# Gated cross-attention kernel: keys stored once, loads by broadcast, the split moved to GpSimd

## The chip, the cores and the metric

The kernel runs on one core of one Trainium2 chip. The metric is the device time of one execution in microseconds (us). A core has TensorE (PE, matmuls into PSUM), VectorE (DVE), ScalarE (ACT), GpSimd (POOL) and SyncE (SP, which here only issues DMAs); 16 DMA engines move the data between HBM and SBUF. Engines meet at semaphores.

## The reference, cut to what matters

```
x = x + tanh(g_xattn) * xattn(layernorm(x), ctx)      # x: 8 x 512 x 256, ctx: 8 x 1601 x 128
x = x + tanh(g_ffn)   * ffn(layernorm(x))

xattn:  q, k, v = x@Wq+bq, x@Wk+bk, x@Wv+bv           # 16 heads of 16
        y  = softmax(causal(q k^T / 4)) v
        qc, kc, vc = x@Wcq+bcq, ctx@Wck+bck, ctx@Wcv+bcv
        y += softmax(qc kc^T / 4) vc
        return y @ Wp + bp
ffn, twice:  weights = softmax over the 2 chosen of 6 experts
        combined  = sum_e weights[e] * (expert_e(xf) + bdown_e)
        share_out = sum over 2 shared experts of (... @ share_Wdown + share_bdown)
        xf = rmsnorm(xf + combined + share_out)
```

The weights of a token's two experts add up to 1.

## The kernel before, in words

A float32 operand is used as a high part of reduced width (the type F32R) and a low part, the difference; products of the two are summed, so that the result keeps float32's precision. The program has four stages, each a block that all engines leave together.

**Projection** (`stage_project`, 8 batches). PE makes queries, keys and values into six PSUM banks, by 23 outputs a batch, ten of them keys. Queries: DVE adds the bias (line 406) and SP stores one row set (`q_rows`). Keys: ACT writes the high part (line 479), DVE reads the same bank again and writes the low part (line 395), and SP stores both parts of every piece (`k_parts`, line 297, 8 DMAs a batch). Values: DVE adds the bias (line 420) and SP stores them at the batch's end (line 314). DVE also makes the low part of the next batch's context (`ctx_low`, line 381, both inputs in SBUF). Towards the end ACT issues the loads of the first item's rows (`First.load_rows`, one DMA for each 16 rows), and GpSimd splits the first item's queries (`split_queries`, lines 114 and 118).

**Attention** (`stage_attend`, 32 items: a batch's four groups of 4 heads). On the contracted axis PE sees 64 rows for each pair of heads: three copies of the 16 rows of a head (queries high, high, low against keys high, low, high), two rows that hold the softmax shift, and rows of zeros. Three key tiles and three query tiles rotate. The order of PE's work is written out by hand, one letter for a piece, and every item takes the same string:

```
ORDER = ("AMSMASMAMSAMSMASMAMSAMSMASMASMOSAMSMASMA"
         "SHAMSMASMAMSAMSMASMAMSAMSMASMAMSAMSMASMA"
         "MSAMSMAASHMASMMSAASMMSMSASMOSA")
```

S are scores (line 893, exponentials by ACT at line 850), A the product with the values (line 908), M the maximum tiles of the next item (line 881, reduced by DVE at line 803), O the output of the item before (self part) or of this one (cross part). H transposes maxima into shift rows: the first H is the self part of this item, the second the cross part of the next. After each H, DVE writes the rows and SP moves them into the query tile with four small DMAs, each from 8 partitions (`shift_rows`, line 687); PE's first scores of that part wait for them. These first cross scores are the last two S of the string.

SP's queue in one item, in this order: keys of item n+2 (`load`, 18 DMAs, line 664), values of n+2, zeros for the scatter rows, a block of x every fourth item (line 722), the self shift of n, queries of n+3 (`load_queries`, 12 DMAs, line 675), the output of n-1 (`store`), the cross shift of n+1. GpSimd's queue: copy of the values of n+1 (line 759), split of the queries of n+2, four causal masks (line 786), the sum of item n's two outputs (line 792).

**Mix** (`stage_mix`): output projection, residual from `XR`, layernorm, routing, preparation of the expert weights and of the bias rows `BR`. **Experts** (`stage_experts`): two layers of routed blocks and of shared passes; a shared down projection begins with a bf16 matmul of a selector row with the bias (line 2051), 64 times in all.

Of the kernel before, what the change touches and what calls it, by code (L numbers as in the profile page):

```python
# [17 lines left out]
P = 128  # L18
# [22 lines left out]
KPART = [0, 1, 0]  # L41
# [65 lines left out]
def written(tag, batches):  # L107

    return (32 if tag[0] in "kc" else 16) * batches + 1


def split_queries(pool, q, raw, s_hi, s_lo, n):

    pool.tensor_copy(q[:, :, :, :], raw[:, :, :, :]).then_inc(s_hi, 1)
    pool.wait_ge(s_hi, n + 1)
    for h in range(2):
        rows = slice(64 * h + 2 * D, 64 * h + 3 * D)
        pool.tensor_tensor(q[rows, :, :, :], raw[rows, :, :, :], q[rows, :, :, :].bitcast(F32), ALU.subtract).then_inc(s_lo, 1)  # L118
    pool.wait_ge(s_lo, 2 * n + 2)
# [45 lines left out]
class First:  # L165


    def __init__(self, r_):
        self.K, self.Q = r_.sb("K0", [P, 2, NKE], F32R), r_.sb("Q0", [P, 2, 2, T], F32R)
        self.qraw = r_.sb("qraw", [P, 2, 2, T])  # L170
# [4 lines left out]
        self.s_qld, self.s_hi, self.s_lo = r_.sem("qld"), r_.sem("qhi"), r_.sem("qlo")  # L175
        self.s_wr = {n: r_.sem("wr_" + n) for n in WRITES}

    def clear(self, pool):

        pool.memset(self.zero[:, :, :, :], 0.0).then_inc(self.s_fill, 1)  # L180
        pool.memset(self.mx[:, :, :], 0.0).then_inc(self.s_fill, 1)
        for h in range(2):
            pool.wait_ge(self.s_fill, h + 2)
            pool.memset(self.K[64 * h + 32:64 * h + 64, :, :].bitcast(F32), 1.0).then_inc(self.s_fill, 1)
        pool.wait_ge(self.s_fill, 4)

# [8 lines left out]
    def load_rows(self, eng, h, r, QS, KS):  # L195

        rows = slice(64 * h + r * D, 64 * h + (r + 1) * D)
        eng.dma_start(self.K[rows, :, 0:NK].bitcast(F32),
                      KS[KPART[r]].rearrange("(i p h d) c -> i h d p c", i=NI, p=2, h=2)[0, h]).then_inc(self.s_ld, 16)
# [8 lines left out]
def stage_project(nc, a, QS, KS, VS, const, first):  # L208
    with ExitStack() as ctx:
# [14 lines left out]
        kpart = r_.sb("kpart", [P, 2, KC, NK], F32R)  # L224
# [30 lines left out]
        NSP = len(split)  # L255

# [12 lines left out]
        r_.prime({s_fin.name: NO})  # L269
        with nc.Block() as block:  # L270

            @block.sync
            def _(sp):
# [11 lines left out]
                def write(b, tag):  # L285
# [4 lines left out]
                    sp.wait_ge(s_fin, NO * (b + 1) + ks[-1] + 2)  # L290
# [4 lines left out]
                    for part in range(2):  # L295
                        row = KS[part].rearrange("(b r) c -> b r c", b=B)[bass.ds(b, 1), cg * P:(cg + 1) * P, c0:c0 + n]
                        sp.dma_start(row.rearrange("o r c -> (o r) c"), tile[:, part, cg, c0:c0 + n].bitcast(F32)).then_inc(s_wr[tag], 16)
# [5 lines left out]
                def body(b, more, more2):  # L303
# [8 lines left out]
                    sp.wait_ge(s_fin, NO * (b + 2) + 1)  # L312
# [11 lines left out]
            def _(pool):  # L324
# [15 lines left out]
                for n in range(4, B):  # L340
                    power(n)
                pool.wait_ge(first.s_qld, 16 * 14)
                split_queries(pool, first.Q, first.qraw, first.s_hi, first.s_lo, 0)

            @block.vector
            def _(dve):
# [36 lines left out]
                def body(b, more):  # L383
                    for k, o in enumerate(outs):
# [7 lines left out]
                        if k in rank:  # L392
                            tile, cg, c0, n, bias = parts(o)
                            dve.wait_ge(s_h, b * NSP + rank[k] + 2)
                            dve.scalar_tensor_tensor(tile[:, 1, cg, c0:c0 + n], bank[:, 0:n], bias,
                                                     tile[:, 0, cg, c0:c0 + n].bitcast(F32), ALU.add, ALU.subtract
                                                     ).then_inc(s_fin, 1)
# [42 lines left out]
            def _(act):  # L440
# [22 lines left out]
                def body(b, more, early=None):  # L463
                    seen = set()
                    for k, o in enumerate(outs):
# [9 lines left out]
                        if o[3] not in seen:  # L475
                            act.wait_ge(s_wr[o[3]], 32 * b + 1)
                            seen.add(o[3])
                        act.wait_ge(s_out, b * NO + k + 2)
                        act.activation(tile[:, 0, cg, c0:c0 + n], acc[k % NBANK][:, 0:n], ACT.Identity,
# [18 lines left out]
            def _(pe):  # L498
# [10 lines left out]
                def body(b, more):  # L509
                    for k, o in enumerate(outs):  # L510
# [10 lines left out]
                        prev = k - NBANK if k >= NBANK else max(i for i in range(NO) if i % NBANK == k) - NO  # L521
                        pe.wait_ge(s_fin, NO * (b + 1) + prev + 2)
# [34 lines left out]

def stage_attend(nc, a, QS, KS, VS, YS, XS, XR, idf, idm, mqm, first, early):

# [5 lines left out]
    with ExitStack() as ctx:  # L565
# [18 lines left out]
        s_ld = [r_.sem(f"ld{u}") for u in range(NU)]  # L584
# [1579 lines left out]
```

## Time and profile before

| | us |
|---|---|
| median of 3 runs | 2416.43 |
| lowest and highest | 2416.25, 2420.34 |
| the profiled execution, its own time | 2420.15 |
| its span, first to last instruction | 2418.1 |

The profiled execution lies 3.7 us over the median, and 2.1 us of its time lie outside its span. Times inside the span count from its start. The stages end at about 213.5, 1575 and 1678 us; the first 39.5 us of attention work on the maxima of item 0.

### The profile page before, as it was taken

How to read it: one execution, taken by the hardware profiler on the slowest of the kernel's cores; microseconds unless marked ns; L12 is line 12 of the kernel's file. 1: busy time of each engine (PE TensorE's matmuls, PEld its weight loads, DVE VectorE, ACT ScalarE, POOL GpSimd, SP SyncE). 2: the span in 40 equal slices, each digit the busy share in tenths (PEclk: the TensorE clock that was granted, in tenths of full speed). 3: DMA queues.
4: the chain of work that ended last, by engine and by line, in shares of the span. 5: the costliest groups of instructions: out<-in, count | busy, mean ns of one | idle time of the engine just before them, and what ended most of it. 6: DMA issues, size and time to landing. Idle time of an engine off the chain costs nothing. (4 is left out here: it accounts for less than half of the span.)

```text
span 2418.1 us, 56126 instructions
## 1 busy us (share of the span) xinstructions
PE 2319.9 (96%) x20518; PEld 1485.7 (61%) x20518; DVE 1892.7 (78%) x3186; ACT 1556.5 (64%) x3328; POOL 814.8 (34%) x631
## 2 busy tenths in 40 slices
PE   7978999999999999999999999988999999999996
PEld 7866444444444444444444444487888888888885
DVE  7869899999999999999999999476633654654747
ACT  3321688888888888888888888854344543533542
POOL 0205343333334242424243332023332423523514
PEclk9997899999999999999999999987999999999998
DMA  7999554545464645454444543262144422422623
GB/s 280 385 338 304 97 101 87 102 77 95 83 98 73 95 82 85 89 86 89 85 86 88 92 73 58 61 213 71 65 137 125 136 68 87 142 70 85 206 82 110
DMA packets 176970, 289.25 MB, mean 120 GB/s; under 512 B 48775, under 2 KB 115470, under 8 KB 175310
## 3 DMA queue, kind: packets, MB, share of 16 engines
q1 hardware_dynamic: 163358, 249.03, 43.7%
q0 software_dynamic: 12288, 33.57, 4.5%
q8 instruction: 166, 2.72, 0.5%
q10 hardware_dynamic: 1072, 3.23, 0.5%
q14 instruction: 86, 0.70, 0.1%
HBM read 165.10 MB, written 119.29 MB: 118 GB/s over the span
## 5 line engine op out<-in xcount | busy, mean ns | idle before, releaser
L850 ACT ACTIVATE at_P<-at_ST 128x512 f32<-128x512 f32 (+4 forms) x2176 | 1091.5, 557 | 233.8 <-PE at_ST L893 189.2
L803 DVE TENSOR_REDUCE f_part<-at_R 128x2 f32<-128x804 f32 x1024 | 953.6, 990 | 43.8 <-PE at_R L881 26.5
L908 PE MATMUL at_OP<-at_P,at_V 128*32 128x256 f32 x8192 | 621.7, 383 | 3.5 <-ACT at_O L858 0.8
L893 PE MATMUL at_ST<-at_Q,at_K 64*128 64x512 f32 (+4 forms) x1428 | 324.8, 428 | 1.3 <-ACT at_P L850 0.9
L908 PEld LDWEIGHTS at_OP<-at_P,at_V 128*32 128x32 f32 x8192 | 172.8, 108 | 248.9 <-ACT at_P L850 186.0
L881 PE MATMUL at_R<-at_K,at_Q 64*128 64x402 f32 x1344 | 273.1, 401 | 0.0
L893 PEld LDWEIGHTS at_ST<-at_Q,at_K 64*128 64x128 f32 (+1 forms) x1428 | 155.0, 181 | 127.5 <-ACT at_P L850 114.5
L800 DVE TENSOR_REDUCE f_mx<-at_R 128x2 f32<-128x256 f32 (+3 forms) x256 | 204.4, 820 | 34.9 <-PE at_R L874 29.3
L786 POOL TENSOR_SCALAR_AFFINE_SELECT at_P<-at_P 128x512 f32<-128x512 f32 x128 | 81.2, 634 | 405.0 <-ACT at_P L850 405.0
L1881 DVE TENSOR_TENSOR ex_ab<-ex_bank,ex_sg 128x256 f32<-128x256 f32 x148 | 62.8, 425 | 195.0 <-ACT ex_sg L1964 177.4
L881 PEld LDWEIGHTS at_R<-at_K,at_Q 64*128 64x128 f32 x1344 | 126.3, 184 | 140.4 <-DVE f_part L803 106.3
L1043 POOL DMA_INDIRECT sorted<-c_XR,c_IDX x128 | 126.7, 989 | 218.4 <-DVE c_bcmp L1119 88.2
L1824 POOL DMA_INDIRECT ex_gb<-expert_rows,c_IDX x128 | 127.0, 992 | 206.7 <-DVE ex_ab L1881 115.4
L118 POOL TENSOR_TENSOR at_Q<-f_qraw,at_Q 16x2048 fp32r<-16x2048 f32 x42 | 191.8, 4568 | 3.3
L1964 ACT ACTIVATE ex_sg<-ex_bank 128x256 f32<-128x256 f32 x148 | 56.8, 384 | 184.6 <-PE ex_bank L100 184.6
L792 POOL TENSOR_TENSOR at_ysum<-at_y 128x256 f32<-128x256 f32 x32 | 23.4, 733 | 443.6 <-DVE at_y L829 443.6
L893 PE MATMUL at_ST<-f_Q,f_K 64*128 64x512 f32 (+4 forms) x748 | 170.2, 430 | 0.5 <-ACT at_P L850 0.5
L881 PE MATMUL at_R<-f_K,f_Q 64*128 64x402 f32 x704 | 151.3, 426 | 9.1 <-DVE f_part L803 6.5
L98 PE MATMUL ex_bank<-c_WH,ex_xbL 128*128 x296 | 143.7, 486 | 0.0
L881 PEld LDWEIGHTS at_R<-f_K,f_Q 64*128 64x128 f32 x704 | 68.8, 192 | 88.7 <-DVE f_part L803 70.4
L893 PEld LDWEIGHTS at_ST<-f_Q,f_K 64*128 64x128 f32 (+1 forms) x748 | 81.3, 183 | 64.6 <-ACT at_P L850 61.2
L100 PE MATMUL ex_bank<-c_WH,ex_xbH 128*128 x296 | 117.0, 395 | 0.0
(250 smaller groups left out, 4425.3 us busy)
## 6 DMA issues: line engine op xcount, KB each, us to landing
k_parts<-pj_kpart SPq DMA_DIRECT2D x32, 800.5 KB, 7.5
f_qraw<-q_rows SPq DMA_DIRECT2D x372, 64.0 KB, 2.8
at_K<-k_parts SPq DMA_DIRECT2D x252, 88.0 KB, 5.2
expert_rows<-ex_rb SPq DMA_DIRECT2D x148, 128.0 KB, 1.7
ex_xb<-sorted SPq DMA_DIRECT2D x72, 256.0 KB, 3.1
v_items<-pj_vbuf SPq DMA_DIRECT2D x8, 2176.0 KB, 11.7
at_K<-k_parts SPq DMA_DIRECT2D x126, 88.1 KB, 5.6
f_K<-k_parts SPq DMA_DIRECT2D x120, 88.0 KB, 5.1
```

The lines of the kernel that those rows point to most:

```text
L98: pe.matmul(out, wL, xH, start=start, stop=False)
L100: return pe.matmul(out, wH, xH, start=False, stop=stop)
L118: pool.tensor_tensor(q[rows, :, :, :], raw[rows, :, :, :], q[rows, :, :, :].bitcast(F32), ALU.subtract).then_inc(s_lo, 1)
L786: pool.affine_select(out=diag, in_=diag, compare_op=ALU.is_ge, fill=0.0, base=0, pattern=[[0, G], [1, P]], channel_multiplier=-1).then_inc ...
L800: dve.tensor_reduce(maxima(SELF)[:, :, p, q], buf[:, :, 0:(q + 1) * P], AX.X, ALU.max).then_inc(s_drain, 1)
L803: dve.tensor_reduce(part[:, :, p, q, c], buf[:, :, 0:XC], AX.X, ALU.max).then_inc(s_drain, 1)
L850: act.activation(Pt[(NKT * n + s) % NP][0:rows, h, c0:T], ST[(NST * n + s * G + h) % NB][0:rows, c0:T], ACT.Exp, scale=SCALE).then_inc(s_e ...
L881: ins = pe.matmul(buf[:, h, 0:XC], Q[u][r0:r0 + 64, CROSS, p, q * P:(q + 1) * P], K[u][r0:r0 + 64, p, at:at + XC], start=True, stop=True)
L893: pe.matmul(ST[t % NB][0:rows, c0:T], K[n % NU][half, p, keys], Q[n % NU][half, kind, p, c0:T], start=True, stop=True).then_inc(s_st, 1)
L908: ins = pe.matmul(OP[32 * h:32 * h + 2 * D, at], V[n % 2][0:rows, key_tile(s), h, :], Pt[(NKT * n + s) % NP][0:rows, h, at], start=s in (0 ...
L1043: pool.indirect_dma_start(XS[h], bass.IndirectOffsetOnAxis(ap=self.IDX[h][:, j, t:t + 1], axis=0), XR[:, h * self.HT + t, :], None).then_i ...
L1824: pool.indirect_dma_start(gb[n % NGB][j][:, :], None, RS[h], bass.IndirectOffsetOnAxis(ap=R.IDX[h][:, j, t:t + 1], axis=0)).then_inc(s_ga[ ...
```

## The change

The keys are stored once, in float32, and so are no longer split in the projection. In attention a raw key tile takes three identical copies of each row set by a broadcast DMA, and GpSimd splits it with two instructions into the tile that PE reads; queries are loaded and split in the same way. A column `low` of 0 and 1 picks the rows that take the low part. One raw tile of each kind serves all items, so its next load waits for the split before it. GpSimd's sum of an item's outputs moves to the next item, between the two splits. SP now issues the keys of item n+3 behind the self shift of n, and the queries behind the store, both ahead of the cross shift of n+1. `load_rows`, for item 0, keeps its DMAs. The blocks of x are loaded in the mix stage. The shared down bias is added, twice, to each expert's down bias, so the matmul at line 2051 goes.

```diff
-KPART = [0, 1, 0]
+KPART = [1, 0, 0]
+def split_rows(pool, out, raw, low, s_hi, s_lo, done):
+    pool.tensor_scalar(out, raw, low, 1.0, ALU.mult, ALU.mult).then_inc(s_hi, 1)
+    pool.wait_ge(s_hi, done)
+    pool.tensor_tensor(out, raw, out.bitcast(F32), ALU.subtract).then_inc(s_lo, 1)
+    pool.wait_ge(s_lo, done)
...
+    def split_keys(self, pool, K, n):
+        split_rows(pool, K[:, :, 0:NK], self.kraw[:, :, 0:NK], self.low[:, 0:1], self.s_hi, self.s_lo, 2 * n + 1)
+    def split_queries(self, pool, Q, n):
+        split_rows(pool, Q[:, :, :, :], self.qraw[:, :, :, :], self.low[:, 1:2], self.s_hi, self.s_lo, 2 * n + 2)
...
@@ projection: SP, GpSimd, DVE
-                    for part in range(2):
-                        row = KS[part].rearrange("(b r) c -> b r c", b=B)[...]
-                        sp.dma_start(row.rearrange("o r c -> (o r) c"), tile[:, part, cg, c0:c0 + n].bitcast(F32)).then_inc(s_wr[tag], 16)
+                    row = KS.rearrange("(b r) c -> b r c", b=B)[...]
+                    sp.dma_start(row.rearrange("o r c -> (o r) c"), tile[:, cg, c0:c0 + n]).then_inc(s_wr[tag], 16)
...
+                pool.wait_ge(s_xn, QT * B + 1)
+                pool.wait_ge(first.s_ld, 16 * 6)
+                first.split_keys(pool, first.K, 0)
                 pool.wait_ge(first.s_qld, 16 * 14)
-                split_queries(pool, first.Q, first.qraw, first.s_hi, first.s_lo, 0)
+                first.split_queries(pool, first.Q, 0)
...
                         if k in rank:
-                            dve.scalar_tensor_tensor(tile[:, 1, cg, c0:c0 + n], bank[:, 0:n], bias, ...
                             continue
@@ attention: SP
                 def load(n):
-                    for r in range(3):
-                        for h in range(2):
-                            for c0, c1 in zip(KCUT, KCUT[1:]):
-                                sp.dma_start(K[u][rows, :, c0:c1].bitcast(F32), KS[KPART[r]]...[n, h, :, :, c0:c1]).then_inc(s_ld[u], 16)
+                    sp.wait_ge(first.s_lo, 2 * n - 1)
+                    src = KS.rearrange("(i p h d o) c -> i p h o d c", i=NI, p=2, h=2, o=1)
+                    for p in range(2):
+                        for h in range(2):
+                            sp.dma_start(first.kraw[64 * h:64 * h + 3 * D, p, 0:NK],
+                                         src[n, p, h].to_broadcast([3, D, NK])).then_inc(first.s_ld, 16)
                 def load_queries(n):
                     sp.wait_ge(first.s_lo, 2 * n)
                     for h in range(2):
-                        for r in range(3):
-                            for kind in range(2):
-                                sp.dma_start(first.qraw[rows, kind], q[n, h, kind]).then_inc(first.s_qld, 16)
+                        for p in range(2):
+                            sp.dma_start(first.qraw[64 * h:64 * h + 3 * D, :, p], q[n, h, p].to_broadcast([3, D, 2, T])
+                                         ).then_inc(first.s_qld, 16)
...
                 shift_rows(0, CROSS)
+                load(2)
                 load_queries(2)
                 for n in range(NI):
                     if n + 2 < NI:
-                        load(n + 2)
                         load_values(n + 2)
                     clear(n)
-                    if n % NG == 1:
-                        sp.dma_start(XR[:, b * QT:(b + 1) * QT, :], ...).then_inc(s_xr, 16)
                     shift_rows(n, SELF)
                     if n + 3 < NI:
-                        load_queries(n + 3)
+                        load(n + 3)
                     if n >= 1:
                         store(n - 1)
+                    if n + 3 < NI:
+                        load_queries(n + 3)
                     if n + 1 < NI:
                         shift_rows(n + 1, CROSS)
@@ attention: GpSimd
+                keys(1)
                 queries(1)
                 for n in range(NI):
                     if n + 1 < NI:
                         values(n + 1)
+                    if n + 2 < NI:
+                        keys(n + 2)
+                    if n:
+                        both(n - 1)
                     if n + 2 < NI:
                         queries(n + 2)
                     ...
@@ mix and experts
+                load_x(0)
                 load_y(1)
+                load_x(1)
...
+                        dve.scalar_tensor_tensor(raw[:, 2, :], sbias[:, :], float(NS), raw[:, 2, :], ALU.mult, ALU.add)
...
-                        pe.matmul(dst, SEL[:, NE, :], BR[:, 2 * C:3 * C], start=True, stop=False)
```

## Rows read from the trace of the kernel before

**Rows 1.** Windows by stage: us; busy PE, PEld, DVE, ACT, POOL; clock; DMA share; GB/s

```profile
0.00:213.50 213.50, 178.29 (x1048) 160.46 (x1048) 167.63 (x382) 71.92 (x112) 32.66 (x34) 0.96 0.94 339
...
253.00:1575.00 1322.00, 1312.51 (x14475) 625.59 (x14475) 1194.73 (x1526) 1123.27 (x2239) 464.92 (x280) 1.00 0.49 85
...
1678.00:2418.00 740.00, 707.78 (x4251) 600.84 (x4251) 416.44 (x1029) 309.85 (x868) 259.50 (x261) 0.98 0.35 109
```

**Rows 2.** A window inside the projection stage

```profile
60.00:70.00 10.00, 10.00 (x56) 8.71 (x55) 9.81 (x25) 2.31 (x3) 1.82 (x2) 1.00 1.01 415
```

**Rows 3.** Timeline of SP in the projection stage

```profile
45.58 1.65 SPq L293 DMA_DIRECT2D q_rows<-pj_qpart  x2
...
66.68 1.65 SPq L293 DMA_DIRECT2D q_rows<-pj_qpart  x2
...
198.87 1.65 SPq L293 DMA_DIRECT2D q_rows<-pj_qpart  x2
```

**Rows 4.** Timeline of SP in one item of attention

```profile
602.12 2.66 SPq L687 DMA_DIRECT2D at_Q<-at_sh  x4
...
620.02 2.66 SPq L687 DMA_DIRECT2D f_Q<-at_sh  x4
...
643.41 2.00 SPq L687 DMA_DIRECT2D f_Q<-at_sh  x3
```

**Rows 5.** Timeline of PE: the first cross scores of the next item

```profile
624.83 0.50 PE L893 MATMUL at_ST<-f_Q,f_K 64*128 64x512 f32 x2
```

**Rows 6.** DMA issues: KB each, median us to landing

```profile
k_parts<-pj_kpart SPq DMA_DIRECT2D x32, 800.5 KB, 7.5
f_qraw<-q_rows SPq DMA_DIRECT2D x372, 64.0 KB, 2.8
at_K<-k_parts SPq DMA_DIRECT2D x252, 88.0 KB, 5.2
...
k_parts<-pj_kpart SPq DMA_DIRECT2D x32, 256.0 KB, 8.7
```

**Rows 7.** DMA packets of 601.5 to 609 us: only the four shift DMAs

```profile
DMA packets 65, 0.03 MB, mean 4 GB/s; under 512 B 32, under 2 KB 64, under 8 KB 64
```

**Rows 8.** DMA packets of 611 to 619.6 us: 12 query loads, one store

```profile
DMA packets 1104, 0.92 MB, mean 107 GB/s; under 512 B 720, under 2 KB 720, under 8 KB 1104
```

**Rows 9.** Timeline of POOL at the end of the projection stage

```profile
184.57 1.89 POOL L114 CAST f_Q<-f_qraw 128x2048 fp32r<-128x2048 f32 x1 [19.94 <-DMA f_qraw<-q_rows]
186.54 9.29 POOL L118 TENSOR_TENSOR f_Q<-f_qraw,f_Q 16x2048 fp32r<-16x2048 f32 x2
```

**Rows 10.** Line 381 alone: its durations in ns, min, median, max

```profile
L381 DVE TENSOR_TENSOR pj_ctxL<-pj_ctxr,pj_ctxH x8: 1806/1814/4379, 16.8 to 193.1; 128x1602 fp32r<-128x1602 f32 x8
```

**Rows 11.** Timeline of POOL in one item of attention

```profile
618.94 0.64 POOL L786 TENSOR_SCALAR_AFFINE_SELECT at_P<-at_P 128x512 f32<-128x512 f32 x1 [7.48 <-ACT at_P L850]
...
624.96 0.64 POOL L786 TENSOR_SCALAR_AFFINE_SELECT at_P<-at_P 128x512 f32<-128x512 f32 x1 [0.55 <-ACT at_P L850]
639.85 0.73 POOL L792 TENSOR_TENSOR at_ysum<-at_y 128x256 f32<-128x256 f32 x1 [14.25 <-DVE at_y L829]
640.52 1.09 POOL L759 COPY at_V<-f_vraw 128x1088 f32<-128x1088 f32 x1
```

**Rows 12.** Windows around PE's stall in the projection stage

```profile
182.00:184.00 2.00, 1.80 (x5) 1.79 (x6) 2.00 (x6) 0.33 (x1) 0.00 (x0) 0.50 0.99 353
184.00:186.00 2.00, 2.00 (x7) 1.90 (x7) 2.00 (x4) 1.25 (x3) 1.43 (x1) 0.50 0.93 365
186.00:188.00 2.00, 2.00 (x14) 2.00 (x14) 2.00 (x5) 0.80 (x2) 1.92 (x2) 0.76 0.91 334
```

**Rows 13.** Instructions of at_Q: first and last start

```profile
L893 PE MATMUL at_ST<-at_Q,at_K x1428: 219/397/504, 294.6 to 1570.2; 64*128 64x512 f32 x136, 64*65 64x512 f32 x11, 64*128 64x384 f32 x11, 64*128 64x128 f32 x11
L881 PE MATMUL at_R<-at_K,at_Q x1344: 335/441/683, 253.1 to 1525.8; 64*128 64x402 f32 x192
```

**Rows 14.** Groups of instructions, the line that goes in the experts stage

```profile
L2051 PE MATMUL ex_bank<-c_BR,c_SEL 96*128 96x256 bf16 x64 | 18.4, 287 | 6.0 <-DVE ex_aL L1860 6.0
```

More of the change, by code:

```diff
@@ L169, in __init__ @@
         self.K, self.Q = r_.sb("K0", [P, 2, NKE], F32R), r_.sb("Q0", [P, 2, 2, T], F32R)
-        self.qraw = r_.sb("qraw", [P, 2, 2, T])
+        self.qraw, self.kraw = r_.sb("qraw", [P, 2, 2, T]), r_.sb("kraw", [P, 2, NKE])
+        self.low = r_.sb("low", [P, 2])
         self.vraw = r_.sb("vraw0", [P, NKT, GC])
@@ L183, in clear @@
             pool.wait_ge(self.s_fill, h + 2)
-            pool.memset(self.K[64 * h + 32:64 * h + 64, :, :].bitcast(F32), 1.0).then_inc(self.s_fill, 1)
+            pool.memset(self.kraw[64 * h + 32:64 * h + 64, :, :], 1.0).then_inc(self.s_fill, 1)
         pool.wait_ge(self.s_fill, 4)
+        pool.memset(self.low[:, :], 0.0).then_inc(self.s_fill, 1)
+        done = 5
+        for kind, parts in enumerate((KPART, QPART)):
+            for h in range(2):
+                r0 = 64 * h + parts.index(1) * D
+                pool.wait_ge(self.s_fill, done)
+                pool.memset(self.low[r0:r0 + D, kind:kind + 1], 1.0).then_inc(self.s_fill, 1)
+                done += 1
+        pool.wait_ge(self.s_fill, done)
+    def split_keys(self, pool, K, n):
+        split_rows(pool, K[:, :, 0:NK], self.kraw[:, :, 0:NK], self.low[:, 0:1], self.s_hi, self.s_lo, 2 * n + 1)
+    def split_queries(self, pool, Q, n):
+        split_rows(pool, Q[:, :, :, :], self.qraw[:, :, :, :], self.low[:, 1:2], self.s_hi, self.s_lo, 2 * n + 2)
     def load_zeros(self, eng):
@@ L255, in stage_project, with finished @@
         NSP = len(split)
+        plain = [k for k, o in enumerate(outs) if o[0] not in "kc"]
+        place = {k: j for j, k in enumerate(plain)}
+        NPL = len(plain)
+        def finished(k, b):
+            return (s_h, NSP * (b + 1) + rank[k] + 2) if k in rank else (s_fin, NPL * (b + 1) + place[k] + 2)
         def parts(o):
@@ L554, in _, with stage_attend @@
                 body(B - 1, False)
-def stage_attend(nc, a, QS, KS, VS, YS, XS, XR, idf, idm, mqm, first, early):
+def stage_attend(nc, a, QS, KS, VS, YS, XS, idf, idm, mqm, first, early):
     with ExitStack() as ctx:
@@ L762, in queries, with keys @@
                 def queries(n):
-                    pool.wait_ge(first.s_qld, 16 * (14 + QLOADS * n))
                     if n >= NU:
                         pool.wait_ge(s_st, NST * (n - NU + 1))
-                    split_queries(pool, Q[n % NU], first.qraw, first.s_hi, first.s_lo, n)
-                ones(1)
+                    pool.wait_ge(first.s_qld, 16 * (14 + QLOADS * n))
+                    first.split_queries(pool, Q[n % NU], n)
+                def keys(n):
+                    if n >= NU:
+                        pool.wait_ge(s_st, NST * (n - NU + 1))
+                    pool.wait_ge(first.s_ld, keys_in(n))
+                    first.split_keys(pool, K[n % NU], n)
                 for n in WRITES:
```

130 lines of the change are left out of this document (52 added, 78 removed).

## The prediction

> **What bounds the kernel now.** I read the windows by stage first. The projection is at its DMAs' limit: 213.5 us with 339 GB/s and a DMA share of 0.94 [rows 1]. Inside it a full stretch moves 415 GB/s at a share of 1.01 [rows 2], so one of the 16 engines moves 25.9 GB/s. The SP timeline tells what a batch costs without that: the shortest distance between two batches' query stores is 21.1 us, while the seven distances from 22.15 to 198.87 average 25.2 [rows 3]. Attention is PE's: 1312.5 of 1322 us, clock 1.00 [rows 1], one item in 41.3 us (the self shifts at 602.12 and 643.41 [rows 4]). PE's order is fixed, so anything that PE waits for is added in full. Its tightest link is the cross shift: SP issues its four DMAs at 620.02 to 622.68 [rows 4], and PE's first scores that read them start at 624.83 [rows 5]. A DMA takes some 2.6 us beyond its transfer (a 64 KB load lands after 2.8 [rows 6], of which 0.2 at 415 GB/s), so there is next to no slack.
>
> **How a load is spread.** In 601.5 to 609 us only the four shift DMAs run, each from 8 source partitions. They leave 32 data packets and 32 small ones, 8 of each per DMA [rows 7]. Beside them 12 query loads to 16 partitions and one store from 128 leave 720 small packets, of which 512 are the store's 256-byte rows: 208 for 13 DMAs, 16 each [rows 8]. I read the small packet as one engine's completion. Then a DMA runs on as many engines, up to 16, as its outer dimension gives: 8 for 8 rows. The new loads' destination has 48 partitions, but their source begins with the broadcast dimension of 3, and a division that fits both gives 3. Bounds: 3 and 16 engines; I take 3, since the 8-row DMAs show the smaller side deciding (their destination is one row of 1024).
>
> The Trainium skill (DMA: Bandwidth & Descriptors, "Why a DMA increments its semaphore by 16 and not by 1") takes the largest number up to 16 that divides both outer dimensions, says that these are the lowest-numbered engines, and in its rules for kernel authors names a leading broadcast of c copies as confining a DMA to c engines. By that rule the new loads run on three engines; the trace agrees on 8 and 16 [rows 7, 8] and holds no case of 3.
>
> **The change, part by part** (against the profiled execution's 2420.15 us, 3.7 over the median).
>
> Projection. 213.5 us at 339 GB/s [rows 1] are 72 MB, 9.0 a batch; the key stores are 32 of 800.5 KB and 32 of 256 KB [rows 6], 4.3 MB a batch, and half of them goes. At 21.1 us a batch the remaining 6.9 MB need 325 GB/s, below the 415 seen. DVE loses ten low parts a batch. I keep the first distance of 23.4 (filling) and set the other six, 153.3 us from 45.58 to 198.87 [rows 3], to 21.1: 126.6, so -26.7. At the end GpSimd now splits item 0's keys before its queries. The query split shows 1.89 us for 2048 elements in one-input form and 4.6 in two-input form [rows 9]; for the keys' 4226 that is 3.9 + 9.4 = 13.3 us, and the queries fall to 1.9 + 4.6 = 6.5, one subtraction in place of two. The split's inputs were there at 184.57, and GpSimd had waited 19.9 us for them [rows 9]. The batch that issues them comes about 13 us earlier (half of the 26.7), and with short queues I take 4 more off: 167, so the split ends near 187, with the stage (213.5 - 26.7). The price of `tensor_scalar` has no row: bounds are the one-input and the two-input rate, 3.9 and 9.4 us; I take 3.9, since it reads one tensor. I book -26, bounds -12 and -32.
>
> One danger lies here. Line 381 takes 1814 ns, but 4379 the one time it met GpSimd's subtraction [rows 10]: begun at 193.14, it ran on past that one's end at 195.83 [rows 9]. The keys' subtraction is a 9.4 us obstacle of this kind; it stands inside the bound of -12.
>
> The Trainium skill (SBUF — State Buffer, "Who interferes with whom") says that a DVE instruction with two SBUF inputs and a GpSimd one that reads SBUF lock each other out for a whole instruction. By it the projection could lose up to 9.4 us more, and attention nothing, because DVE's instructions there have at most one input in SBUF; rows 10 agree for the first, and no row quoted here shows the second.
>
> Attention, GpSimd. Its queue gets, an item, values 1.1 + keys 13.3 + sum 0.7 + queries 6.5 before the masks. It is free at 625.6 behind the last mask and needs until about 649 (PE's products with values a little later than the mask included), and the next first mask would come at 618.94 + 41.3 = 660.2 [rows 11]: 11 us of slack, 3 if both `tensor_scalar` cost the two-input rate. I book 0. The sum's move is hidden as well: its store is waited for two items later.
>
> Attention, the loads. Their bytes don't change: 18 x 88 KB and 12 x 64 KB [rows 6], 1.62 and 0.79 MB. Three engines carry 77.8 GB/s: 20.9 and 10.1 us. SP now issues both between the self shift of n and the cross shift of n+1. With the self shift's issue as zero [rows 4]: its DMAs are out at 2.7, the keys (the split before them being done) follow, the queries behind them; all has landed at 2.7 + 2.6 + 31.0 = 36.3. The cross shift is issued at 17.9 as before, but its packets stand behind the loads on the three engines, which it also uses. It lands at 36.5 instead of before 22.7, and **PE waits 13.8 us an item**. After a stall PE works at half clock: in the projection line 395 and its like began again at about 182, and the clock was still 0.50 to 186 and 0.76 on average to 188 [rows 12]: some 4.8 us at half speed, 2.4 lost. Together 16.2 us an item, for n = 1 to 28 (no key load follows item 31): 28 x 16.2 = 454. Bounds per item: 12 (clock free) and 27 (engines a third slower when alone).
>
> Attention, the first items. Against the stage's start T (213.5 before): loads of item 1 land at T + 34.3, splits end at T + 54.1, and PE wants item 1's maxima at 253.1 [rows 13], T + 39.6: +14.5. The keys of item 2 wait for that key split (T + 47.6), their own split ends at T + 84.4, and SP holds the keys of item 3, their queries and the cross shift of item 1 behind it: landing at T + 118. PE wanted it at 294.6 [rows 13], T + 81.1. So +37 for n = 0, the 14.5 included. SP's queue is blocked there by the wait for the split: behind it stand the store and the cross shift.
>
> Mix and experts. The x blocks come from a DMA in the stage, needed well behind its start: 0 to 3, I take +1. One broadcast and one DVE operation on the bias: 0. Line 2051 goes 64 times. Its group's 18.4 us overlap other matmuls [rows 14]; the stage's 4251 matmuls take 707.8 us [rows 1], 0.17 each, so 64 are 10.7. This one is bf16 and 256 wide, narrower than most: -6, bounds 0 and -11.
>
> **Sum:** 2420.15 - 26 + 37 + 454 + 1 - 6 = 2880 us, 19% slower.
>
> **The rivals.**
> (1) The loads use all 16 engines after all, by their 48 partitions. Then keys and queries have landed at 2.7 + 2.6 + 5.8 = 11, before the cross shift is issued, and what stays is 2420.15 - 26 - 6 + 1 = 2389, faster. The point that decides is the landing at 22.7: 2.41 MB in 17.4 us are 138 GB/s, between five and six engines. For it: I have no row with 3. Against it: rows 7.
> (2) Three engines, but small DMAs overtake the loads. Then only the first items' 14.5 stay: 2404. Against it: nothing in the trace lets a later DMA pass.
> (3) Three engines, each slower alone than in a full stretch, or a clock that recovers later: each us more costs 28; a fifth slower is 6 us or 174: 3050 and up.
> (4) The gain of the projection is eaten by a lock or a late load, with (1): 2420.
>
> **How the numbers follow.** The forecast has 0.72, rival (1) 0.15, (2) 0.02, (3) 0.09, (4) 0.02. The predicted time is the forecast's. Its own range is 2720 to 3060 by the bounds above; to 3180 it takes in most of (3) and holds nearly 8 in 10. The two faster cases stay outside. Faster by over 0.2% (what a measurement here can tell): 0.17; within: 0.02; slower: 0.81.
>
> **What would show it.** Small packets per broadcast load: 3, against 16. In attention DMA share near 0.2 while loads run; PE idle 14 us an item in front of line 893, ended by the DMA at_Q<-at_sh, clock below 1.00, items of 57 us. In the projection, query stores 21 us apart and a stage end near 187. GpSimd: 3.9 + 9.4 us for a key split. I am wrong if the items stay at 41.3 us.

## The result: 3127.53 us, and the profile after

The changed kernel took 3127.53 us (median of 4 runs, 3116.30 to 3131.04) against 2416.51 us for the kernel before on the same chip. The ratio is 1.293, with a 95% interval of 1.291 to 1.295. The direction and the mechanism were forecast, and 2880 was 8% short. The profiled execution is the 3116.30 us one, with a span of 3114.6; before it was 2420.15 us. All of the loss lies in attention. Windows by stage of the kernel after, in the columns of [rows 1]:

```profile
0.00:190.50 190.50, 173.37 (x1048) 159.83 (x1048) 124.64 (x302) 71.43 (x112) 44.83 (x40) 0.99 0.85 298
237.00:2260.00 2023.00, 1352.22 (x14332) 643.52 (x14332) 1193.78 (x1521) 1116.24 (x2211) 737.40 (x309) 0.82 0.17 53
2370.00:3114.00 744.00, 707.67 (x4229) 605.25 (x4229) 422.81 (x1047) 314.31 (x877) 268.94 (x270) 0.98 0.36 110
```

The projection stage ends at 190.5 in place of 213.5. Attention's row is 2023 us long where [rows 1] has 1322. PE's busy time in it hardly grew, its clock fell to 0.82, and the DMA share is 0.17 on average. What PE waited for is in the waits view (engine, line, what it waited for; us in total, times, the longest):

```profile
PE at_ST L906 <- DMA at_Q<-at_sh: 445.4, 20, 27.5
PE at_ST L906 <- DMA f_Q<-at_sh: 210.7, 11, 23.8
PE at_R L894 <- POOL at_Q L116: 15.7, 1, 15.7
```

656.1 us over 31 waits end with the shift DMA. The third row is the split of item 1, once. One item in full, on SP (start and duration, us), which answers to [rows 4]:

```profile
1844.39 2.69 SPq L699 DMA_DIRECT2D f_Q<-at_sh  x4
1847.13 3.04 SPq L678 DMA_DIRECT2D f_kraw<-k_rows  x4
1850.22 0.58 SPq L704 DMA_DIRECT2D y_rows<-at_ysum  x1
1850.85 25.58 SPq L686 DMA_DIRECT2D f_qraw<-q_rows  x4
1876.47 4.28 SPq L699 DMA_DIRECT2D at_Q<-at_sh  x4
...
1909.04 2.69 SPq L699 DMA_DIRECT2D at_Q<-at_sh  x4
```

and PE's first score that reads the cross shift:

```profile
1889.17 0.79 PE L906 MATMUL at_ST<-at_Q,at_K 64*128 64x512 f32 x2 [22.04 <-DMA at_Q<-at_sh]
```

The self shift is issued at 1844.39 and the cross shift can be used at 1889.17, which is +44.8 where it was +22.7 before [rows 4, 5] and 36.5 was forecast. PE had stood for 22.0 us. The four query loads alone kept SP for 25.58 us, where a DMA's issue otherwise takes 0.7. Windows through the same item:

```profile
1857.00:1863.00 6.00, 5.92 (x74) 2.93 (x74) 5.35 (x9) 4.85 (x10) 0.64 (x1) 1.00 0.20 63
1869.00:1875.00 6.00, 0.00 (x0) 0.00 (x0) 0.00 (x0) 0.00 (x0) 0.00 (x0) 0.50 0.18 69
1887.00:1891.00 4.00, 1.83 (x18) 1.31 (x18) 0.32 (x1) 1.00 (x2) 0.00 (x0) 0.50 0.08 31
1891.00:1895.00 4.00, 3.98 (x42) 1.72 (x44) 3.14 (x5) 2.99 (x7) 1.90 (x2) 0.79 0.00 0
1895.00:1899.00 4.00, 4.00 (x46) 1.75 (x46) 3.88 (x6) 3.53 (x7) 3.92 (x2) 1.00 0.02 4
```

While the loads run, 0.18 to 0.20 of sixteen engines are busy, three, and they move 63 to 69 GB/s, all transfers included, and not the 77.8 of the sum. The granted clock is at half (1.2 GHz) while PE stands and stays there for some 4 us after its restart. The packet row of the DMA view, for the 64 us of one item (1842 to 1906):

```profile
DMA packets 1468, 3.45 MB, mean 54 GB/s; under 512 B 664, under 2 KB 728, under 8 KB 1240
```

Its small packets are counted against another kernel's below.

### The profile page after: what moved, and what is told of

Its sections match the earlier page's. It is cut to its first block and busy times, and to the rows that moved or that the text cites. A ratio compares the mean times of both kernels' runs of the same rounds, so it can differ in the third digit from the quotient of the medians.

```text
span 3114.6 us, 55137 instructions
## 1 busy us (share of the span) xinstructions
PE 2360.8 (76%) x20454; PEld 1506.2 (48%) x20454; DVE 1848.8 (59%) x3107; ACT 1561.7 (50%) x3328; POOL 1079.5 (35%) x663
## 5 line engine op out<-in xcount | busy, mean ns | idle before, releaser
L906 PE MATMUL at_ST<-at_Q,at_K 64*128 64x512 f32 (+4 forms) x1428 | 332.9, 448 | 446.3 <-DMA at_Q<-at_sh 445.4
L921 PE MATMUL at_OP<-at_P,at_V 128*32 128x256 f32 x8192 | 642.4, 396 | 3.3 <-ACT at_O L871 0.8
L894 PE MATMUL at_R<-at_K,at_Q 64*128 64x402 f32 x1344 | 276.6, 407 | 15.7 <-POOL at_Q L116 15.7
L116 POOL TENSOR_TENSOR at_K<-f_kraw,at_K 128x4226 fp32r<-128x4226 f32 x21 | 193.9, 9236 | 1.7
L759 POOL COPY at_V<-f_vraw 128x1088 f32<-128x1088 f32 x16 | 17.5, 1092 | 380.7 <-PE at_OP L921 380.7
L759 POOL COPY at_V<-at_vraw 128x1088 f32<-128x1088 f32 x16 | 17.5, 1092 | 362.1 <-PE at_OP L921 362.0
```

The source lines that it names most:

```text
L116: pool.tensor_tensor(out, raw, out.bitcast(F32), ALU.subtract).then_inc(s_lo, 1)
L894: ins = pe.matmul(buf[:, h, 0:XC], Q[u][r0:r0 + 64, CROSS, p, q * P:(q + 1) * P], K[u][r0:r0 + 64, p, at:at + XC], start=True, stop=True)
L906: pe.matmul(ST[t % NB][0:rows, c0:T], K[n % NU][half, p, keys], Q[n % NU][half, kind, p, c0:T], start=True, stop=True).then_inc(s_st, 1)
L921: ins = pe.matmul(OP[32 * h:32 * h + 2 * D, at], V[n % 2][0:rows, key_tile(s), h, :], Pt[(NKT * n + s) % NP][0:rows, h, at], start=s in (0 ...
```

## Where the 696 us come from

SP's self shifts are the clock of attention. Those of items 0, 1 and 29 in the kernel after, and the cross shift behind the last:

```profile
280.25 3.72 SPq L699 DMA_DIRECT2D f_Q<-at_sh  x4
...
349.28 2.65 SPq L699 DMA_DIRECT2D at_Q<-at_sh  x4
...
2171.30 2.69 SPq L699 DMA_DIRECT2D at_Q<-at_sh  x4
2189.16 2.67 SPq L699 DMA_DIRECT2D f_Q<-at_sh  x4
```

From the self shift of item 1 (349.28) to that of item 29 (2171.30) 28 items take 65.07 us each. Before it is 41.3 [rows 4]. The cross shift behind 2171.30 comes 17.86 us later, as before: there no load stands in between. The self shift of item 1 stands 158.8 us behind the start of the stage, and 99.7 before (313.18 - 213.5 in the timeline of SP). From the self shift of item 29 to the end are 943.3 us, against 948.5 before (from 313.18 + 28 x 41.3 = 1469.6 to 2418.1).

| part | predicted | measured |
|---|---|---|
| projection | -26 | -23 |
| first items | +37 | +59.1 |
| 28 items | 28 x 16.2 = +454 | 28 x 23.8 = +665.6 |
| mix and experts | +1 - 6 = -5 | -5.2 |
| sum from 2420.15 | 2880 | 3116.6 (3116.3 measured) |

## The experiments

Where a run has a single time, that time is its profiled execution's. The items' lengths are means over the 28 items from the self shift of item 1 to that of item 29, as above; the changed kernel has 65.07.

The kernel before was timed beside every group of runs. It took 2413.73 to 2422.76 us beside the first four experiments, 2415.44 to 2421.59 beside the half rows and the last experiment, and 2416.33 beside the rows 32 partitions apart. But beside the other four (queries by copy, ScalarE's cross shift, the cross shift ahead of the loads, copies 0 and 1 in pairs) its only execution took 2472.31 us, 55 more than usual. It left no trace, but the four show the like: from the last self shift (item 31) to the end they take 909 to 915 us, all other kernels here 860 to 867, the changed kernel 862. No edit touches that part, so 47 to 52 us of each of these four times have nothing to do with the experiment. Their items can be compared, their totals only with this in mind.

### One DMA per copy

```
-                    for p in range(2):
-                        for h in range(2):
-                            sp.dma_start(kraw[64h : 64h+48, p, 0:NK], src[n, p, h].to_broadcast([3, D, NK]))
+                    for r in range(3):
+                        for h in range(2):
+                            sp.dma_start(kraw[64h+16r : 64h+16r+16, :, 0:NK], src[n, h])
```

The queries are treated likewise, 12 DMAs in place of 4.

> One DMA per copy of 16 rows (6 for the keys, 12 for the queries of an item) in place of four broadcasts each; all else as in the changed kernel. Three-engine theory: each load runs on 16 engines again, cross shifts land some 23 us after the self shift's issue, items fall from 67.4 to 41.3 us, DMA rate while loads run is far above 77.8 GB/s, the time is 2385 (2370 to 2405). Rival, the split on GpSimd or its waits cost the time: it stays above 3000 and GpSimd's key splits end late. Rival, the store-once loads are slow by their byte count: no change either.

Measured: 2524.13 us (5 runs, ratio 1.043, interval 1.041 to 1.045). So 603 of the 711 us of loss (3127.53 - 2524.13, of 3127.53 - 2416.51) go with the number of engines, and the rivals (GpSimd's split, SP's waits, the bytes, all unchanged) fall. But it is not 2385: items take 45.4 us. SP, a window, and PE in this kernel:

```profile
1028.99 2.66 SPq L700 DMA_DIRECT2D at_Q<-at_sh  x4
1031.95 2.68 SPq L678 DMA_DIRECT2D f_kraw<-k_rows  x6
...
1035.30 5.97 SPq L687 DMA_DIRECT2D f_qraw<-q_rows  x12
1046.86 2.67 SPq L700 DMA_DIRECT2D f_Q<-at_sh  x4
```

```profile
1033.00:1053.00 20.00, 18.84 (x220) 9.22 (x218) 17.56 (x23) 15.44 (x34) 3.46 (x5) 1.00 1.05 131
```

```profile
1054.67 0.79 PE L907 MATMUL at_ST<-f_Q,f_K 64*128 64x512 f32 x2 [1.82 <-DMA f_Q<-at_sh]
```

All sixteen engines are busy (share 1.05), and together they move only 131 GB/s, a third of the 415 of [rows 2]. The cross shift is issued on time, 17.9 us after the self shift, but lands at +25.7. Its 8452-byte packets take 1059 ns on average, against 320 to 330 for one that runs undisturbed. The kernel before does the same in its own key loads, to which no row of the prediction went:

```profile
626.00:640.00 14.00, 13.96 (x146) 6.48 (x147) 13.33 (x17) 12.69 (x24) 0.15 (x1) 1.00 1.04 121
```

The limit of such a load is thus neither the number of engines nor HBM (415 GB/s were seen with both). What these loads have in common is 16 neighbouring partitions as their destination. The Trainium skill (SBUF — State Buffer, "Door 1: The DMA port swizzle") says that DMA bandwidth depends on how many of 16 ports the partitions reach, with four neighbours on one port. By it 16 neighbours reach four ports, and with that page's 436 GB/s for all 16 a load into them gets 109 GB/s by estimate. The 121 and 131 measured lie 11% and 20% above that, other transfers included; the six key loads by themselves bring 1.62 MB in 13.6 us on average, 119 GB/s. The next experiment brings the same key bytes, on sixteen engines too, into 48 partitions a load, in 10.1 us. That fits a limit set by the partitions; no run varies the partitions alone.

### The copy as the inner dimension

```
-                            sp.dma_start(kraw[64h : 64h+48, p, 0:NK], src[n, p, h].to_broadcast([3, D, NK]))
+                            sp.dma_start(kraw[64h : 64h+48, p, 0:NK], src[n, p, h].to_broadcast([D, 3, NK]))
```

Row d's copy r now lies in partition 3d + r of its half, so the mask `low` and `load_rows` use every third partition. Queries likewise, with `qraw` laid out as pair, kind, column.

> The same 8 broadcasts an item, but the copy is the second dimension of the source (16 rows, 3 copies, the row) and row d's copy r lies in partition 3d + r of its half, so the outer dimension is 16. Three-engine theory: 16 small packets per load, items of 41.3 us, 2385 (2365 to 2405), within 0.5% of one DMA per copy. Rival, a broadcast is slow in itself, since it reads each row three times: it stays near 3116.

Measured: 2391.11 us (4 runs, ratio 0.988, interval 0.987 to 0.990). The same eight broadcasts, the same bytes and the same splits, and the time is 26.6 us under the kernel before. Items are at 41.30 us. It beats both kernels. SP and a window:

```profile
1033.17 2.66 SPq L701 DMA_DIRECT2D at_Q<-at_sh  x4
1035.87 2.54 SPq L680 DMA_DIRECT2D f_kraw<-k_rows  x4
...
1039.09 2.55 SPq L688 DMA_DIRECT2D f_qraw<-q_rows  x4
1051.03 2.76 SPq L701 DMA_DIRECT2D at_Q<-at_sh  x4
```

```profile
1035.00:1053.00 18.00, 17.92 (x204) 8.37 (x206) 16.86 (x23) 15.43 (x31) 4.79 (x3) 1.00 0.86 144
```

SP is no longer held: four query loads issue in 2.55 us. Packets of one item:

```profile
DMA packets 1382, 3.48 MB, mean 84 GB/s; under 512 B 768, under 2 KB 832, under 8 KB 1152
```

768 small packets against 664 in the changed kernel: 104 more, that is 8 loads x (16 - 3). So a load leaves 16 completions here and left 3 there, and the reading of [rows 7, 8] by which the source's leading 3 sets the number of engines holds.

### The bias change alone

Kernel before, with the shared experts' down bias added once to the routed rows' bias, and line 2051 gone.

```
-                        pe.matmul(dst, SEL[:, NE, :], BR[:, 2 * C:3 * C], start=True, stop=False)
                         for c in range(KC):
                             ins = mm3(pe, dst, aH[:, c, tok], aL[:, c, tok], dH[:, NE, c, :], dL[:, NE, c, :],
-                                      False, c == KC - 1)
+                                      c == 0, c == KC - 1)
```

> The kernel before with the shared down bias in the routed rows alone. By the prediction's term: 64 narrow bf16 matmuls less, -6 us (0 to -11), 2410 against 2416.4. Rival: they lay beside other work and nothing moves, 2416.

Measured: 2413.84 us against 2417.73 (ratio 0.998, interval 0.997 to 0.999), -3.9 us with an interval of -7 to -3. The experts stage shows it, 734 us and 4188 matmuls where [rows 1] has 740 and 4251:

```profile
1678.00:2412.00 734.00, 700.98 (x4188) 598.20 (x4187) 416.26 (x1031) 309.89 (x868) 260.33 (x261) 0.98 0.35 110
```

### Keys by copy, queries by broadcast

The keys' half of the first diff, the queries' broadcasts left as they are:

```
-FIRST, LOADS, QLOADS = 6, 4, 4
+FIRST, LOADS, QLOADS = 6, 6, 4
```

> Keys by six DMAs of 16 rows, queries still by four broadcasts. Three-engine theory: the queries need 10.1 us on three engines, begin at some 6 us after the self shift's issue and have landed by 21 us, ahead of the cross shift's 22.7: no stall, items of 41 to 43 us, 2390 (2380 to 2440). Rival, broadcasts hurt by being issued at all (SP blocked in issuing the queries whatever stands ahead): the 27 us of issue stay, items above 55, 2800 and more.

Measured: 2722.88 us, items of 52.1. A miss. SP:

```profile
999.67 2.77 SPq L678 DMA_DIRECT2D f_kraw<-k_rows  x6
...
1003.45 11.06 SPq L686 DMA_DIRECT2D f_qraw<-q_rows  x4
1014.82 5.04 SPq L699 DMA_DIRECT2D f_Q<-at_sh  x4
```

The expectation took 4 us for the keys by copy. At 121 GB/s their 1.62 MB need 13.4, and only then come the queries' 10 on three engines: 2.7 + 2.6 + 13.4 + 10.1 is 29, 6 over the limit of 22.7. The measured excess of an item is 10.8. PE's waits for shifts are 260.9 us in 29 waits, 9.0 each, where this sum has 6; the clock adds to them, and the rest is not resolved further. What decided here was the rate into 16 partitions, again. SP's issue shrank from 26 to 11 us, so the rival, that issuing a broadcast blocks SP whatever stands ahead, falls too.

### Queries by copy, keys by broadcast

The other half:

```
-FIRST, LOADS, QLOADS = 6, 4, 4
+FIRST, LOADS, QLOADS = 6, 4, 12
```

> Queries by twelve DMAs of 16 rows, keys still by four broadcasts. Three-engine theory with the measured keys (29 us on the slowest of the three): all has landed at 35 us after the self shift's issue, the cross shift at 36.5 in place of 46.5, items of 57.5 us in place of 67.4, 2840 (2780 to 2900). With three engines at the full 25.9 GB/s each the keys would need 20.9, items of 49 and 2600. Rival, most of the wait comes from the queries' broadcasts: items under 50 us, 2550 or less.

Measured: 3053.53 us, items of 61.0. A miss in size, also without the 47 us.

```profile
1023.62 2.81 SPq L700 DMA_DIRECT2D f_Q<-at_sh  x4
1026.48 3.03 SPq L678 DMA_DIRECT2D f_kraw<-k_rows  x4
...
1030.20 28.06 SPq L687 DMA_DIRECT2D f_qraw<-q_rows  x12
1058.30 2.78 SPq L700 DMA_DIRECT2D at_Q<-at_sh  x4
```

```profile
1066.07 0.80 PE L907 MATMUL at_ST<-at_Q,at_K 64*128 64x512 f32 x2 [19.66 <-DMA at_Q<-at_sh]
```

PE can use the cross shift at +42.5 (1066.07 - 1023.62), not +36.5. SP is held in issuing the queries for 28 us, although thirteen of the engines that they use have no keys to carry, so the cross shift is issued at +34.7. Nor do the keys get away with 29 us: the queries' packets now run beside them into the same partitions, the key packets' mean is 453 ns (395 in the changed kernel), and the last of this item's ends 33.6 us behind the start of the first. The expectation had priced neither. What holds SP was not tried by itself.

### ScalarE issues the cross shift

Loads unchanged. The four DMAs of the cross shift leave SP's queue for ScalarE's.

```
 # SP
-                    if n + 1 < NI:
-                        shift_rows(n + 1, CROSS)
 # ScalarE, two exponentials behind the SHIFT event of (n, CROSS)
+                    act.wait_ge(s_drain, slot["SHIFT", n, CROSS] + 1)
+                    for h in range(2):
+                        for r in range(2):
+                            row = 64 * h + KROWS + r
+                            act.dma_start(Q[n % NU][row:row + 1, CROSS].bitcast(F32),
+                                          sh[CROSS][2 * QT * h:2 * QT * (h + 1), r].bitcast(F32)).then_inc(s_shd[CROSS], 16)
```

> Cross shifts issued by ScalarE, in its own queue, two exponentials after their place; loads unchanged. Theory A, the cross shift waits behind the loads in SP's queue (27 us of issue and the packets ahead in it): out of that queue it lands within 5 us of its issue, items of 42 to 46 us, 2420 (2390 to 2530). Theory B, the engines are the shared thing and serve in order of issue over all queues: it waits for the loads all the same, items above 55 us, 2800 and more.

Measured: 2646.11 us, items of 47.1. SP is held as before, and an item's loads still take 39 us:

```profile
1033.84 2.80 SPq L699 DMA_DIRECT2D at_Q<-at_sh  x4
1036.68 3.05 SPq L678 DMA_DIRECT2D f_kraw<-k_rows  x4
...
1040.40 26.83 SPq L686 DMA_DIRECT2D f_qraw<-q_rows  x4
```

```profile
PE at_ST L918 <- DMA at_Q<-at_sh: 54.4, 20, 4.2
PE at_ST L918 <- DMA f_Q<-at_sh: 28.6, 11, 5.4
```

PE's 656 us of waits for shifts become 83. Out of SP's queue the cross shift passes the loads; the engines that both use are not the obstacle, the place in SP's queue is. The time is 116 us over the range, of which 52 lie behind attention. The 39 us of loads stand in one queue with the next self shift; with the 5.3 us from a shift's issue to the first byte behind it that makes 44 of the item's 47 us, so it is the loads' own length that is left. The expectation had left it out.

### SP issues the cross shift ahead of the loads

```
-                        load(n + 3)
                     if n >= 1:
                         store(n - 1)
-                    if n + 3 < NI:
-                        load_queries(n + 3)
                     if n + 1 < NI:
                         shift_rows(n + 1, CROSS)
+                    if n + 3 < NI:
+                        load(n + 3)
+                        load_queries(n + 3)
```

> SP issues the cross shift ahead of the key and query loads; they are unchanged. By queue order the cross shift lands 5 us after its issue, but the loads then take until 42 us behind it: the next self shift lands at 44 where PE can use it at 37, and the splits of those loads (13.3 and 6.5 us) end on GpSimd at 52, ahead of the item's masks. Items of 50 (self shift decides) to 60 us (masks decide), 2630 to 2900, I take 2850. Rival, the order is of no account: 3116.

Measured: 2806.90 us, items of 52.7. The stall moved to the next self shift, now the one that stands behind the loads:

```profile
1040.07 2.68 SPq L699 DMA_DIRECT2D f_Q<-at_sh  x4
1042.79 3.11 SPq L678 DMA_DIRECT2D f_kraw<-k_rows  x4
1045.94 23.55 SPq L686 DMA_DIRECT2D f_qraw<-q_rows  x4
...
1076.60 3.15 SPq L699 DMA_DIRECT2D f_Q<-at_sh  x4
```

```profile
1087.22 0.80 PE L906 MATMUL at_ST<-f_Q,f_K 64*128 64x512 f32 x2 [8.37 <-DMA f_Q<-at_sh]
```

DVE had its rows ready at 1064.7, but SP issued the self shift only at 1076.60, and PE can use it 47.2 us behind the issue of the cross shift, where the expectation had 44. Over the run PE's waits for shifts are 218.9 us in 31 waits. GpSimd's key split waits as well, for its load (23.8 us in this item), but PE waits for GpSimd only once, at item 1 (15.7 us). So of the two bounds of the expectation it is the self shift that decides (50 us) and not the masks (60). Order alone buys 12.4 us an item of the 23.8 and no more. As long as the loads run on three engines, something stands behind them.

### Half of each key row

Broadcasts of the first half of the columns only; the second half keeps item 0's keys, so this kernel does not compute the other items' attention in full.

```
-                            sp.dma_start(kraw[64h : 64h+48, p, 0:NK], src[n, p, h].to_broadcast([3, D, NK]))
+                            sp.dma_start(kraw[64h : 64h+48, p, 0:NK//2], src[n, p, h, :, :, 0:NK//2].to_broadcast([3, D, NK//2]))
```

> The changed kernel, with the broadcasts of the keys cut to the first half of their columns from item 1 on (the second half keeps item 0's keys, so the attention of the others isn't computed in full); everything else, the splits too, is the same. By the transfer time on the path: the keys' 29 us fall to 14.5, items from 65 to 50.5, 2700 (2660 to 2740). Rival, the stall hangs on SP's issue or on a wait for GpSimd and not on bytes: items stay over 60 us, 3000 and more.

Measured: 2692.20 us, items of 51.1. The stall goes by bytes. Removing half of the keys took 14.0 us from an item, so all of them would cost 28.0 us of it at this price, where the sum had 20.9; in the changed kernel their packets span 27.4. Keys and queries together took 36.6 to 41.0 us from the first key packet to the last query packet in the 24 items of the changed kernel between 450 and 2100 us, 39.1 on average: 2.41 MB at 61.6 GB/s, 20.5 for each engine. Forecast were 31.0 and 25.9.

### Why the three are slow: copies 0 and 1 in pairs

```
+                            sp.dma_start(kraw[64h : 64h+32, p, 0:NK], src[n, p, h].to_broadcast([2, D, NK]))
+                    sp.dma_start(kraw[64h+32 : 64h+48, :, 0:NK], src2[n, h])     # for each h
```

> Copies 0 and 1 of the keys by broadcasts of two (partitions 0 to 31 and 64 to 95), copy 2 by one DMA of 16 rows; queries as in the changed kernel. Each of two engines carries 64 packets of 8452 bytes an item from the broadcasts, as each of three did. Theory A, the slow packets come from two engines that write partitions 0 to 15 and 32 to 47 at once: here no such pair is left, packets take some 325 ns on both, keys done 21 to 23 us after their start, items of some 60 us, 2920. Theory B, reading the same row from several engines slows them: means stay near 400 ns on all but one, keys take 27 to 29 us, 3100.

Measured: 3164.32 us, items of 64.9, where the changed kernel has 65.07. SP's last self shift is at 2252.56 us here and at 2252.42 there, so the 48 us between 3164.32 and the changed kernel's 3116.30 all lie behind attention. Without them the time is near theory B's 3100. But it is not there for B's reason, as the packets show. In the changed kernel the 8452-byte packets of one moment are mostly of two kinds: 320 to 331 ns, or some 600 to 680 ns, two overlapping at a time. In all 14% lie between 600 and 700, and their mean is 395. Here copy 2's DMA fills some 6 us near the start (packets of 1000 ns and more on all sixteen), and behind it, with two engines left, the mean is 331 ns at first and 341 later. So two engines at copies 0 and 1 don't slow each other, which speaks for theory A over B. The 6 us of copy 2 gave the gain back: the keys took 27.1 us, and 27.4 in the changed kernel. The changed kernel's own slow packets also stand almost all in the first half of an item's key packets (725 of 799 over 550 ns in 25 items; means of 447 and 342 ns in the halves). In the second half most packets of the three engines take 320 to 331 ns, so their number alone doesn't slow them.

### Why the three are slow: rows 32 partitions apart

As the last one, but from item 4 on the first head pair's broadcasts go to every second partition of a half in a spare tile. The keys of that pair stay item 3's in copies 0 and 1.

```
-                            sp.dma_start(kraw[64h : 64h+32, p, 0:NK], ...)
+                            sp.dma_start(kraw[64h : 64h+32, p, 0:NK] if p or n < 4 else aside[64h : 64h+64 : 2, 0:NK], ...)
```

> The kernel of the two-copy run (3164 us, its two engines' 8452-byte packets 325 ns once copy 2 had passed), but from item 4 on the broadcasts of the first head pair go to every second partition of a half in a tile that nothing reads: the two copies' rows then lie 32 partitions apart, as copies 0 and 2 do in the changed kernel, in place of 16. The second pair's broadcasts stay where they were (the keys of the first pair stay item 3's in copies 0 and 1, so its scores are others). Theory A, two engines that write partitions 32 apart share a way into SBUF and halve each other: packets of 400 to 680 ns in the first half of an item's key packets and 325 in the second, keys 4 to 8 us longer, 3280 (3220 to 3400). Theory B, the 640 ns packets of the changed kernel come from three engines reading one row or from the number of engines: 325 ns in both halves, 3164.

Measured: 3160.41 us, items of 66.3, where the last kernel has 64.9. That 3160 is so near 3164 is an accident: the last kernel's time holds some 48 us from behind attention and this one's doesn't. SP's last self shift is at 2298.65 us here and at 2252.56 there, so attention ends 46 us later. Theory A, set against 3164, wanted 116 more (56 to 236), theory B none; by attention the result stands between them, just under A's range. Behind copy 2's DMA the first half of an item's key packets has a mean of 358 ns and the second 342; the last kernel had 331 and 341. Packets of 500 to 680 ns do appear where the 32-apart rows begin, two to six of them, and then the two engines fall out of step and run at 320. The keys take 28.8 us in place of 27.1. The effect has the sign of theory A and less than half of its size. The Trainium skill (SBUF — State Buffer, "Door 1: The DMA port swizzle") puts partitions 32 apart on one port, as copies 0 and 2 are in the changed kernel, and pairs of 640 ns beside a third engine at 320 are what this would look like. With every second partition only two neighbours fall on one port, so the engines would get free of each other sooner; this reading was not tried. That the three-engine broadcast runs at 20.5 in place of 25.9 GB/s an engine is measured; that the cause is a shared port is supported and not settled.

### One DMA per copy, with the queries behind the cross shift

```
                         load(n + 3)
                     if n >= 1:
                         store(n - 1)
-                    if n + 3 < NI:
-                        load_queries(n + 3)
                     if n + 1 < NI:
                         shift_rows(n + 1, CROSS)
+                    if n + 3 < NI:
+                        load_queries(n + 3)
```

> One DMA per copy of 16 rows, as in the run of that kind that took 2524 us, but the queries of n+3 are issued behind the cross shift of n+1 in place of ahead of it. Theory A, a load into 16 neighbouring partitions passes at 114 to 120 GB/s in all, so that keys and queries (2.41 MB) need 21 us, too long for the 17.9 us between the shifts; the keys alone (1.62 MB, 14 us) fit, and the queries (7 us) fit behind: items back at 41.3 us, 2395 (2385 to 2410). Theory B, the 45 us items of that run come from the number of DMAs or from GpSimd's splits: items stay at 45, 2520.

Measured: 2405.55 us (4 runs, ratio 0.995, interval 0.993 to 0.997), items of 41.4. The 45 us items of the first experiment came from 2.41 MB at 119 to 131 GB/s in a 17.9 us gap. With 1.62 MB in it they are gone, with the same DMAs and the same splits.

## Why the prediction was right, and where it was off

**Number of engines:** right, by 104 completions of difference, a share of 0.18 to 0.20, and 2391 against 3128 us for a reordered broadcast.

**PE waits for the cross shift behind the loads:** right. [rows 5] now carries a wait of 22.04, and a second queue takes it away.

**The rate of an engine:** the step that failed. The sum took the 25.9 GB/s of a full stretch [rows 2] for each of three engines and 31.0 us for the loads. They take 39.1. With it the term "28 x 16.2 = 454" was mis-sized: 28 x 23.8 = 666 is measured, and this is 212 of the 236 us between forecast and profiled execution. This is rival (3) come true, which had 0.09: 20.5 GB/s is a fifth below 25.9. The rival's own price was short, since a rate a fifth lower takes a quarter longer, 8 us and not 6. An undisturbed packet does run at the sum's rate (8452 bytes in 324 ns are 26 GB/s). What the sum lacked are first of all the packets of double length: a mean of 395 ns makes 4.5 us over the 64 key packets of an engine. The other 3.6 us of the loads are not resolved, and why the packets are slow is left open above. The range of the sum, 2720 to 3060, was missed. The result lies only inside the one widened to 3180 for rival (3), which is also where the bound of 27 us an item leads (2880 + 28 x 10.8 = 3182). Part of it works the other way: PE's busy time in attention rose by 40 us (1382.3 between 190.5 and 2260 us, 1341.9 between 213.5 and 1575 before), 1.4 an item where 2.4 were set for the clock. From PE's restart to the next self shift are 19.9 us in the item shown, and 18.6 before [rows 4, 5].

**First items:** +59 in place of +37. The split of item 1 held PE for 15.7 us (14.5 forecast); the rest are two passes behind loads, where three engines were reckoned at the full rate.

**Projection:** -23 for -26. The six distances between query stores from 44.70 to 175.36 take 21.8 us, not 21.1. GpSimd at the end of the stage, which answers to [rows 9]:

```profile
168.49 3.84 POOL L114 TENSOR_SCALAR f_K<-f_kraw,f_low 128x4226 fp32r<-128x4226 f32 x1 [16.79 <-DMA f_kraw<-k_rows]
172.42 10.80 POOL L116 TENSOR_TENSOR f_K<-f_kraw,f_K 128x4226 fp32r<-128x4226 f32 x1
183.31 1.99 POOL L114 TENSOR_SCALAR f_Q<-f_qraw,f_low 128x2048 fp32r<-128x2048 f32 x1
185.39 4.60 POOL L116 TENSOR_TENSOR f_Q<-f_qraw,f_Q 128x2048 fp32r<-128x2048 f32 x1
```

The inputs were there at 168.5 (167 forecast), `tensor_scalar` runs at the one-input rate, and the split ended at 190.0 (187). The danger of [rows 10] came in small: the keys' subtraction took 10.80 here and 9.2 in attention, and the longest of DVE's line 404 (line 381 before) is 2808 ns.

**GpSimd in attention** costs nothing, as booked: it waits for ScalarE before the first mask of an item, 11.1 us in one. **Mix and experts:** -5.2 for -5.

**Rival (1)**, all 16 engines, named 2389, and the reordered broadcast took 2391. But its working was wrong in the same place as the sum: it let the loads pass at 415 GB/s and land at 11. Its deciding point was right: 138 GB/s between issue and the landing at 22.7. One DMA per copy moves 131 and misses it, the 48-partition broadcast moves 144 and meets it, both by a few per cent. Sixteen engines alone were not enough.

## What to carry to other kernels

Read a DMA's rate from a stretch in which that kind of DMA runs, with its share beside it: a share near 1.0 at 120 GB/s, as here, says that the engines wait for something else, and the full stretch of another stage says nothing about it. When copies are to be broadcast, put the copy inside and the rows outside, so that the outer dimension is 16 and the destination spreads over many partitions; the same eight DMAs then gained 1% in place of losing 29%. And price a small urgent DMA by all the bytes that stand ahead of it in its own queue.

## What was not expected of the hardware

Loads into 16 neighbouring partitions pass at 119 to 131 GB/s with all sixteen engines busy. The kernel before lived with this (share 1.04), since only its queries stood between self and cross shift. An issuing engine can be held by its own DMAs: SP stood 25.6 us in issuing four broadcasts behind four others, and 2.55 us for the same four when sixteen engines took them.
